# Layer norm of the first attention pass: rows and statistics one tile per slot, the store moved to the next round's beginning

## What is computed

```python
x = x + 0.5 * _L0_ffn_ref(_layernorm(x), ...)     # two layers of local attention and a gated MLP

# one of these two layers
h = shift_token(x)                 # the second half of the columns comes from the row before
qkv = h @ wqkv                     # q, k, v: 8 heads of 64
q, k = l2norm(q) * qs, l2norm(k) * ksc, then rotary
o = local_attention(q, k, v)       # windows of 128 rows, each sees itself and the one before
x = x + o @ wo
```

## Time and profile before

| | |
|---|---|
| median of the runs | 3006.18 us |
| profiled execution | 3008.27 us, span 3006.4 us |
| PE busy | 2915.1 us (97%) |
| DVE, ACT, POOL busy | 78%, 58%, 58% |
| chain that ended last | PE 83%, DVE 7%, POOL 4%, issue 3% |
| granted TensorE clock | 0.994 on average |

### The profile page before, as it was taken

How to read it: one execution, slowest core, us unless ns; L and a number is a source line. 1 busy time by engine, 2 the same in 40 slices (tenths; PEclk the granted TensorE clock), 3 DMA queues, 4 the chain that set the end, 5 groups by cost and what they waited for, 6 DMA issues and landing times.

```text
span 3006.4 us, 95582 instructions
## 1 busy us (share of the span) xinstructions
PE 2915.1 (97%) x34238; PEld 2544.9 (85%) x34238; DVE 2330.4 (78%) x6549; ACT 1743.6 (58%) x4600; POOL 1755.4 (58%) x2008
## 2 busy tenths in 40 slices
PE   6999999999999999999999999999999999999899
PEld 5888888878888888887788888878888888888788
DVE  6888887677777877887777787777777877877777
ACT  4777752267777324776777772257777522554445
POOL 7878740088887234333888861058888455547632
PEclk9999999999999999999999999999999999999999
DMA  4121121012211101000121121111211200000001
GB/s 142 45 73 43 47 81 39 25 35 54 57 42 42 46 21 44 12 12 23 37 69 43 39 68 58 30 27 41 69 41 43 67 21 8 29 1 1 1 15 42
DMA packets 178763, 122.65 MB, mean 41 GB/s; under 512 B 27532, under 2 KB 175336, under 8 KB 178024
## 3 DMA queue, kind: packets, MB, share of 16 engines
q1 hardware_dynamic: 177432, 117.77, 14.5%
q10 hardware_dynamic: 1104, 1.90, 0.2%
HBM read 48.29 MB, written 20.98 MB: 23 GB/s over the span
## 4 chain that ended last, share of the span: by engine, by line
PE 83%; DVE 7%; POOL 4%; issue 3%; DMA 1%; SPq 1%; ACT 1%; DVEq 0%; POOLq 0%; ACTq 0%
PE bank L386 7%; PE bank L388 7%; PE bank L387 7%; PE pair_bank L606 6%; PE scores L558 5%; PE scores L386 5%; PE scores L387 5%; PE scores L388 5%; PE bank L524 3%; PE pair_bank L386 2%; PE pair_bank L871 2%; PE pair_bank L870 2%; PE pair_bank L869 2%; PE scores L820 2%; PE scores L819 2%
## 5 line engine op out<-in xcount | busy, mean ns | idle before, releaser
L2925 POOL TENSOR_TENSOR prob<-prob,rsum 128x384 f32<-128x384 f32 x504 | 446.6, 913 | 233.1 <-DVE rsum L2094 233.1
L1365 ACT ACTIVATE prob<-prob,nmax 128x192 f32<-128x192 f32 x1024 | 452.0, 443 | 153.4 <-DVE nmax L2088 153.4
L1609 ACT ACTIVATE gate<-scores,bias 128x512 f32<-128x512 f32 x192 | 132.1, 689 | 499.3 <-PE scores L388 499.2
L2912 POOL TENSOR_TENSOR rn<-ss,mhalf 128x16 f32<-128x16 f32 x122 | 357.6, 2931 | 10.2
L386 PE MATMUL bank<-wqkv_hi,hT_hi 128*128 128x512 f32 x768 | 334.7, 436 | 8.0 <-DVE rot_t L2043 3.8
L2919 POOL TENSOR_TENSOR qk<-rot_t 128x512 f32<-128x512 f32 x256 | 322.4, 1280 | 18.1 <-DVE ss L2055 15.5
L2088 DVE CUSTOM_DVE_ANT_0 prob<-scores,masks,rn 128x192 f32<-128x192 f32 x768 | 267.6, 414 | 70.2 <-PE scores L558 67.1
L388 PE MATMUL bank<-wqkv_hi,hT_lo 128*128 128x512 f32 x768 | 305.4, 398 | 0.0
L387 PE MATMUL bank<-wqkv_lo,hT_hi 128*128 128x512 f32 x768 | 303.4, 395 | 0.0
L2893 POOL TENSOR_TENSOR rstd<-meanvar,eps 128x4 f32<-128x4 f32 x48 | 11.0, 229 | 488.1 <-DVE meanvar L1993 488.1
L386 PE MATMUL scores<-gT_hi,w_hi 128*128 128x512 f32 x576 | 227.6, 395 | 1.7 <-DVE gT_lo L2338 1.3
(11 more groups left out here) (375 smaller groups left out, 9611.8 us busy)
## 6 DMA issues: line engine op xcount, KB each, us to landing
Vlo<-V SPq DMA_DIRECT2D x256, 64.0 KB, 2.0
Vhi<-V SPq DMA_DIRECT2D x256, 64.0 KB, 2.0
H<-Y SPq DMA_DIRECT2D x128, 64.0 KB, 1.8
H<-ya SPq DMA_DIRECT2D x128, 64.0 KB, 1.9
yb<-Y SPq DMA_DIRECT2D x128, 64.0 KB, 1.6
HB<-Y SPq DMA_DIRECT2D x32, 256.0 KB, 2.8
HB<-yb SPq DMA_DIRECT2D x32, 256.0 KB, 3.1
raw<-in_L_ffn_wqkv SPq DMA_DIRECT2D x4, 1536.0 KB
```

The source lines that it names most:

```text
L1365: e.activation(pb, pb, ACT.Exp, bias=nm[r][:, x:x + 1], scale=-1.0, accum_out=sums[r][:, x:x + 1]).then_inc(s_acEX[gi], 1)
L2912: e.tensor_tensor(rn[u][:, :], ss[u % 2][:, :], mhalf[:, :], ALU.pow).then_inc(s_plRN, 1)
L2925: e.tensor_tensor(pair, pair, rs[:, 2 * gi:2 * gi + 2].unsqueeze(2).to_broadcast([P, 2, KW]), ALU.mult).then_inc(s_plPN[gi], 1)
```

## The change

On VectorE each slot of rounds 0 to 4 now ends with one BN_STATS of group it+3, and each slot of rounds 1 to 5 with one TENSOR_SCALAR of group it+2. In round 0 the rows go to slots 1 to 3, two tiles in slot 1. The four BN_AGGR stand at the end of slot 3, behind the last TENSOR_SCALAR. GpSimd's program is the same, and it still waits at the end of slot 3. On SyncE the store of group it+1 stands at the beginning of round it, for rounds 1 to 6. In the first slot of such a round the value copies and the store to `yb` come before the load, and the wait for the landing of the store stands between them and the load.

```diff
+            def ln_stats_of(n, u):
+                i = e.bn_stats(stats[0][:, u, :], tile(X, U * n + u))
+                if u == U - 1:
+                    i.then_inc(s_lndvST, 1)
+
+            def ln_aggregate(n):
+                e.wait_ge(s_lndvST, n + 2 + OFF)
+                e.sem_inc(s_passed, 1)
+                e.wait_ge(s_lndvXN, U * n + OFF)
+                e.sem_inc(s_passed, 1)
+                for u in range(U):
+                    i = e.bn_aggr(meanvar[0][:, u, :], stats[0][:, u, :])
+                i.then_inc(s_lndvAG, 1)
+
+            def ln_rows(n, rows):
+                e.wait_ge(s_lnplRV, 2 * n + 4 + OFF)
+                e.sem_inc(s_passed, 1)
+                for u in rows:
+                    e.tensor_scalar(tile(Y, U * n + u), tile(X, U * n + u), ...).then_inc(s_lndvXN, 1)
...
                 def extra(it, u):
-                    if run == 0 and u == 1 and not (isinstance(it, int) and it > GRP - 3):
-                        ln_norm(it + 2)
-                    if run == 0 and u == U - 2 and not (isinstance(it, int) and it > GRP - 4):
-                        ln_stats(it + 3)
+                    statistics = run == 0 and not (isinstance(it, int) and it > GRP - 4)
+                    if statistics:
+                        ln_stats_of(it + 3, u)
+                    if run == 0 and not (isinstance(it, int) and it > GRP - 3):
+                        if not (isinstance(it, int) and it == 0):
+                            ln_rows(it + 2, (u,))
+                        elif u:
+                            ln_rows(2, ((0, 1), (2,), (3,))[u - 1])
+                    if statistics and u == U - 1:
+                        ln_aggregate(it + 3)
...
                 def iteration(it):
-                    if run == 0 and not (isinstance(it, int) and it > GRP - 2):
-                        ln_stored(it + 1)
+                    stored = run == 0 and not (isinstance(it, int) and it > GRP - 2)
+                    if stored and isinstance(it, int) and it == 0:
+                        ln_stored(1)
+                    elif stored:
+                        ln_store(it + 1)
                     for u in range(U):
-                        slot(U * it + u, u)
+                        if u == 0 and stored and not (isinstance(it, int) and it == 0):
+                            copies(U * it, 0)
+                            ln_stored(it + 1)
+                            ld(run, U * it + 4, 0)
+                        else:
+                            slot(U * it + u, u)
                         extra(it, u)
-                        if run == 0 and u == 2 and not (isinstance(it, int) and it > GRP - 3):
-                            ln_store(it + 2)
```

More of the change, by code:

```diff
@@ L1932, in ln_norm @@
                     e.tensor_scalar(tile(Y, U * n + u), tile(X, U * n + u), meanvar[r][:, u, 0:1], rstd[r][:, u:u + 1], ALU.subtract, ALU.mult).then_inc(s_lndvXN, 1)
+            def ln_stats_of(n, u):
[14 more added lines that the diff above has]
+                for u in rows:
+                    e.tensor_scalar(tile(Y, U * n + u), tile(X, U * n + u), meanvar[0][:, u, 0:1], rstd[0][:, u:u + 1], ALU.subtract, ALU.mult).then_inc(s_lndvXN, 1)
             FIRST = (range(0, 1), range(1, U))
@@ L3417, in vs_, with copies @@
                             e.dma_start(Vleft[u % 2][half_][rr, cc], V[u][DH * half_:DH * half_ + DH, cc]).then_inc(s_vs[u], 16)
-                def slot(T, u):
-                    if inside(T + 4):
-                        ld(run, T + 4, (u + 4) % U)
+                def copies(T, u):
                     if inside(T - 1):
@@ L3425, in slot @@
                         wo_(run, T - 3, (u - 3) % U)
+                def slot(T, u):
+                    if inside(T + 4):
+                        ld(run, T + 4, (u + 4) % U)
+                    copies(T, u)
                 def iteration(it):
-                    if run == 0 and not (isinstance(it, int) and it > GRP - 2):
-                        ln_stored(it + 1)
-                    for u in range(U):
-                        slot(U * it + u, u)
+                    stored = run == 0 and not (isinstance(it, int) and it > GRP - 2)
[3 more added lines that the diff above has]
+                        ln_store(it + 1)
+                    for u in range(U):
+                        if u == 0 and stored and not (isinstance(it, int) and it == 0):
[4 more added lines that the diff above has]
+                            slot(U * it + u, u)
                         extra(it, u)
-                        if run == 0 and u == 2 and not (isinstance(it, int) and it > GRP - 3):
-                            ln_store(it + 2)
                 def first_in_linear():
```

## The result

The changed kernel took 3035.74 us, the median of four runs (3032.49 to 3037.69), beside 3005.56 us for the kernel before (the median of four runs here, 3004.04 to 3010.15). The ratio is 1.0097, with a 95% interval of 1.0085 to 1.011. So it is about 1% slower; 3037 was predicted.

The account below looks back on a forecast made before the run. TensorE, busy 97% of the span, was taken as the bound, so its waits decide. Terms -12.6 + 1.0 + 29.7 + 12.6 = +30.7 us on 3008.3 made 3039.0; 3037 was predicted for the runs, range 3022 to 3048.

Parts of the forecast that it names:

- The wait for the copies: First slots of rounds 1 to 6: TensorE idles 4.95 us for value copies queued behind SyncE's store wait, 29.7 us together.
- The clock: TensorE's granted clock falls after each of the six waits, costing 2.1 us each, 12.6 us together.
- The bursts: First attention pass, rounds 0 to 5: VectorE's bursts of rows and statistics go, 12.6 us less.
- The rows beside GpSimd's additions: A TENSOR_SCALAR may meet GpSimd's second addition in slots after long TensorE waits: 0.2 us in each of five, 1 us.
- rival of the caught rows: GpSimd's second addition catches each row in 17 slots: 9.5 us instead of 1 us, 3045 us; chance 0.10.
- GpSimd's reciprocals: Waiting for BN_AGGR makes GpSimd about 1 us late in slot 0; counted as nothing, 0.5 us a round without cover.

Follow-up runs that it names:

- busy wait: Changed kernel plus 36 matmuls with unused results on TensorE, ahead of the copies' wait in first slots of rounds 1 to 6; 3031.04 us, ratio 1.0081.
- copies first: Changed kernel, but in rounds 1 to 6 SyncE issues value copies and `yb` store before waiting for and storing the rows; 2998.51 us, again 2999.03.

## Why the prediction was right, step by step

- *The wait for the copies.* Forecast 4.95 us in six rounds, 29.7. Measured: products 5.97, 6.21, 6.25, 6.36, 6.31 and 5.78 us after their slots, less 1.39 each, 28.5. The store follows the row by 0.32 us and not by 0.46; the rest of the chain was within 0.05. Shown by moving the copies (all of it goes), by leaving the rows early (all of it goes), and by ending the rows 3 us earlier (0.2 to 0.4 is left, 1.3 behind the weight loads, nothing in round 6).
- *The clock.* Forecast a fall at each wait, 2.1 us each, 12.6. There were six falls. The six slots grew by 37.3 us, of which the waits are 28.5 - 1.1 = 27.4 (1.1 us of wait was there before, behind the weight loads), so 9.9 are left; the busy wait took 9.2 away. The term was about a third too large, because five of the six falls were as short as the shorter of the two in the earlier trace rows.
- *The bursts.* Forecast -12.6: measured -9.6 in rounds 1 to 5, -1.5 in round 0 and the 1.1 at the weight loads, -12.2.
- *The rows beside GpSimd's additions.* Forecast 1 us. In the profile after, each row of slots 0 to 2 in rounds 1 to 5 did end with the first addition, 0.15 to 0.23 us after it: the row of slot 1 in round 1 takes 0.78 us and ends at 119.77, the addition at 119.62. No slot was longer for it. Slot 2 of round 1 alone took 12.25 us, 1.0 over the rest, with 0.8 us idle as "issue" before L606 on TensorE, which stands at the same place in the kernel before, beneath the burst; its cause is not shown. So the rows cost nothing, and that 1 us is found in this place all the same is luck. The rival of the caught rows was wrong for one row a slot and right for two.
- *GpSimd's reciprocals.* They were counted at nothing because of the wait, with 0.5 us a round if the cover went. The cover did hide them. Without it they alone cost 0.7 (round 5 with the copies first), so the mechanism was right and the size a little small.
- *What the sum left out.* VectorE's aggregation and the end of its loop stood in no term. They bring the scores 2.57 us after slot 0 of round 2, as costly there as GpSimd's lateness. TensorE's wait hid this too in the changed kernel; it was seen only with the copies first.

The sum was 30.7 against 26.2 in the profiled execution: the waits were 1.2 us too high, the clock 2.7, the rows 1.0, and the bursts' gain, which is taken off, 0.4 too high. That the medians of 3035.74 and 3033.41 lay only 1.3 and 3.6 us under the 3037 forecast is therefore in part luck: the first was 30.2 us over the kernel before beside it, the second 26.4.

## What to carry to other kernels

Work that is levelled ends later, and whoever waits for the last piece of it waits longer; look at what is queued behind that waiter on its own engine before placing it. Here 12 us of waiting for VectorE's bursts were won, and some 27 us of waiting behind a transfer queue and 10 us of slower clock lost; exchanging two calls on SyncE turned 1% slower into 0.3% faster. When a slot stays long after one cause is taken away, look whether a second one ends at the same moment. Put extra work where the engine is already waiting in the middle of a slot, not at a loop's end, where the jump's time has to fit as well.

## What the runs showed of the hardware

- A TENSOR_SCALAR on VectorE from SBUF to SBUF that starts beside a GpSimd instruction and would end before it ends 0.15 us after it, if that is an addition of 128x512 (1.28 us), the 128x1024 one of 2.41 us, or a scaling of 128x384. It is not held by the power of 128x16 elements: 0.40 or 0.41 us in its midst, 20 times of 20. The Trainium skill, SBUF — State Buffer, section "Who interferes with whom", has the lock held for the whole instruction; the runs agree for the long operands and not for this one. That the power holds it only while it reads and writes its 16 columns would explain it, but no run shows it.
- A TENSOR_SCALAR that waits gets in between two GpSimd instructions that follow each other at once, one per boundary: the two rows of 0.71 and 1.36 us above.
- The jump back at the end of VectorE's loop body costs 0.80 to 0.83 us in which the engine waits for nothing, if no wait covers it.
- TensorE's clock fell to 1.2 GHz about the end of each of the idle times of 3.6 to 4.8 us that these runs had in first slots, for 3.4 us mostly and 6.8 at times. It did not fall where 36 matmuls whose results nobody uses ran for 4.6 us of the wait, with at most 0.54 us idle behind them, nor behind the idle time of 1.31 us. But long idle times are not the only occasion: in the later passes it also fell without an idle time over 2 us, in the kernel before at 629 us, behind three of 1.07, 0.24 and 0.74.
